# Attention over pairs of heads: values projected untransposed for two heads at once, raw weights kept where their lower parts go

## The reference

```
x = x + attn(layernorm(x), Wq, Wk, Wv, Wg, Wo)      # 8 batches, 512 tokens, 16 heads of 128
x = x + ffn(layernorm(x), ...)                      # top 128 tokens of each batch

q, k, v = h @ Wq, h @ Wk, h @ Wv ; q, k = rope(q), rope(k)      # rope: t*cos + swapped halves*sin
g_cmp, g_slc, g_swa = sigmoid(h @ Wg)                           # one gate per head and token
o_cmp = softmax over 8 block means of k, times block means of v
o_slc = softmax over the causal row, times v                    # all 8 blocks are selected
o_swa = softmax over the last 65 keys, times v
o = g_cmp*o_cmp + g_slc*o_slc + g_swa*o_swa ; return o @ Wo
```

## Time and profile before

| | us |
|---|---|
| median of 3 runs | 2504.64 |
| the profiled execution | 2504.16 |
| its span in the trace | 2502.3 |
| PE busy | 2428.0 |
| DVE busy | 1901.3 |
| POOL busy | 1584.8 |
| ACT busy | 1409.8 |

### The profile page before, as it was taken

The page is one execution under the profiler, slowest core; times in us unless marked ns, Lnnn a source line. Parts: engine busy times, 40 slices in busy tenths (PEclk is TensorE's granted clock), DMA queues, the critical chain, the costliest instruction groups (busy, mean ns, idle before and its releaser), DMA issues. The chain is left out here.

```text
span 2502.3 us, 48659 instructions
## 1 busy us (share of the span) xinstructions
PE 2428.0 (97%) x12944; PEld 2066.0 (83%) x12944; DVE 1901.3 (76%) x5863; ACT 1409.8 (56%) x3808; POOL 1584.8 (63%) x1198
## 2 busy tenths in 40 slices
PE   6999999999999999999999999999978999999998
PEld 5788888888888888888888888888867888887776
DVE  7588888888888888888888888888882777775123
ACT  7566666666666666666666666666652222213442
POOL 1777777777777777777777777777753333333442
PEclk9999999999999999999999999999989999999999
DMA  4222212121222222222222222222225333432366
GB/s 153 60 71 55 75 50 75 50 75 50 75 63 63 63 63 63 62 64 62 64 71 54 71 54 71 54 71 54 58 72 188 133 115 121 155 110 76 102 180 215
DMA packets 145681, 211.78 MB, mean 85 GB/s; under 512 B 14960, under 2 KB 56176, under 8 KB 144624
## 3 DMA queue, kind: packets, MB, share of 16 engines
q1 hardware_dynamic: 145648, 211.37, 28.9%
HBM read 93.87 MB, written 50.33 MB: 58 GB/s over the span
## 5 line engine op out<-in xcount | busy, mean ns | idle before, releaser
L526 PE MATMUL bank<-xt_hi,w_hi 128*128 (+1 forms) x1536 | 619.3, 403 | 3.0 <-PEq L170 0.8
L526 PE MATMUL bank<-xt_hi,w_lo 128*128 (+1 forms) x1536 | 600.8, 391 | 0.0
L526 PE MATMUL bank<-xt_lo,w_hi 128*128 (+1 forms) x1536 | 598.1, 389 | 0.0
L501 POOL TENSOR_TENSOR qk_lo<-s_full,qk_hi 128x512 fp32r<-128x512 f32 x256 | 330.1, 1290 | 274.9 <-ACT qk_hi L621 274.9
L489 POOL TENSOR_TENSOR cosed<-s_full,rope 128x512 f32<-128x512 f32 x256 | 330.6, 1292 | 134.0 <-ACT s_full L610 130.6
L497 POOL TENSOR_TENSOR s_full<-cosed,s_swap 128x512 f32<-128x512 f32 x256 | 333.6, 1303 | 36.7
L526 PEld LDWEIGHTS bank<-xt_hi,w_lo 128*128 128x128 f32 x1536 | 288.2, 188 | 64.1
L526 PEld LDWEIGHTS bank<-xt_hi,w_hi 128*128 128x128 f32 x1536 | 289.2, 188 | 56.6 <-DVE w_lo L138 3.5
L526 PEld LDWEIGHTS bank<-xt_lo,w_hi 128*128 128x128 f32 x1536 | 289.5, 188 | 52.7
L494 POOL TENSOR_TENSOR s_swap<-s_swap,rope 128x512 f32<-128x512 f32 x256 | 332.9, 1300 | 0.1
L626 ACT ACTIVATE pt_hi<-bank 128x384 fp32r<-128x384 f32 (+1 forms) x384 | 174.7, 529 | 260.7 <-PE bank L568 260.5
(11 more groups left out here) (166 smaller groups left out, 5416.9 us busy)
## 6 DMA issues: line engine op xcount, KB each, us to landing
s_swap<-s_full SPq DMA_DIRECT2D x512, 128.0 KB, 2.3
o_scratch<-o_sb SPq DMA_DIRECT2D x128, 256.0 KB, 2.3
o_raw<-o_scratch SPq DMA_DIRECT2D x32, 1024.0 KB, 6.3
w_raw<-in_L_ffn_W SPq DMA_DIRECT2D x64, 256.0 KB, 3.1
xin<-in_L_attn_x SPq DMA_DIRECT2D x15, 1024.0 KB, 5.5
base_scratch<-x SPq DMA_DIRECT2D x8, 1024.0 KB, 4.7
base<-base_scratch SPq DMA_DIRECT2D x32, 256.0 KB, 4.3
out<-base SPq DMA_DIRECT2D x32, 256.0 KB, 3.3
```

The lines of the kernel that those rows point to most:

```text
L501: nc.gpsimd.tensor_tensor(qk_lo[k][:], s_full[k][:], f32(qk_hi[k][:]), ALU.subtract).then_inc(lo_done[k], 1)
L526: last = nc.tensor.matmul(banks[QB[k]][:, :], w[k][:, c, :], v[:, bass.ds(b, 1), c, :], start=(n == 0), stop=(n == 3 * C - 1))
```

## The change

Units are taken in pairs of heads: pair p, then batch b, then head s of the pair, u = p*16 + b*2 + s. What is done for each is this:

- Values: in unit (b, s) the token tiles 2s and 2s+1 of the layer norm stand still and the value weights of both heads stream, 256 columns. That gives tokens by dims directly, for two tiles and two heads, in bank 7. `vt`, its copy and the four transposes are gone. `v_hi` and `v_lo` have five slots of two tiles.
- Banks: the second group of transposed probabilities goes to bank 5, not 7. TensorE waits for the evacuation of k before it and of q before the third group; the projection of values waits for the low parts of the values of the unit before.
- Rope: the cosine product is written in place, so GpSimd waits for the swapped halves first, and q is turned to its end before k. The output tile `o_sb` is now `s_swap[1]`: SyncE waits for the store before it swaps k.
- ScalarE copies the output first in its body, then empties q; the high part of q comes straight after the first row's exponentials.
- Weights: each raw tile of q and k lies where the low part goes, which is then taken in place. There are two sets (one per head of the pair), loaded once per pair in units 14 and 15; the value weights are one tile of 256 columns per chunk. VectorE splits q, GpSimd k and the values.
- Gates of all heads are stored to DRAM and loaded back 16 units at a time (`gates_dram`).
- `normalise` splits four tiles of q and k and the double tile of v on GpSimd before the attention begins, where there were three tiles.
- Loops: TensorE's loop over pairs has 16 bodies written out. The other engines have a loop over pairs with four bodies written out (`quad`), and inside it a loop of three rounds over four bodies.

```diff
+            def project_values(b, s):
+                for i in range(2):
+                    out = banks[7][:, :].rearrange("p (a i d) -> p i a d", a=2, i=2)[:, i]
+                    at = (2 * s + i) * P
+                    n = 0
+                    for c in range(C):
+                        for x, w in ((xt_hi, weights.v_hi), (xt_hi, weights.v_lo), (xt_lo, weights.v_hi)):
+                            last = nc.tensor.matmul(out, x[:, b, c, at:at + P], w[:, c, :],
+                                                    start=(n == 0), stop=(n == 3 * C - 1), skip_group_check=True)
+                            n += 1
+                last.then_inc(projected[2], 1)
...
-                    project_one(b, 2)
-                if score:
-                    pe.wait_ge(evacuated[2], u)
-                    if end:
-                        pe.wait_ge(pt_lo_done, (u - 2) * 3 + 2)
-                    for t in range(T):
-                        last = nc.tensor.transpose(banks[7][:, t * P:(t + 1) * P], vt[:, t * P:(t + 1) * P], m("ident"))
-                    last.then_inc(v_transposed, 1)
+                    pe.wait_ge(weights.v_split, p * 2 + 2)
+                    if not begun:
+                        pe.wait_ge(v_lo_done, u)
+                    project_values(b, s)
...
+            with pe.Fori(1, PAIRS) as p:
+                for k in range(4):
+                    quad(p, k)
...
 (GpSimd)
-            def turn_cos(u, k):
+            def turn(u, k):
                 pool.wait_ge(evacuated[k], u + 1)
-                nc.gpsimd.tensor_tensor(cosed[k][:], s_full[k][:], rope[:, 0, :], ALU.mult).then_inc(cos_done[k], 1)
-            def turn_sin(u, k):
                 pool.wait_ge(swapped[k], u * 32 + 32)
+                nc.gpsimd.tensor_tensor(s_full[k][:], s_full[k][:], rope[:, 0, :], ALU.mult).then_inc(cos_done[k], 1)
                 nc.gpsimd.tensor_tensor(s_swap[k][:], s_swap[k][:], rope[:, 1, :], ALU.mult).then_inc(sin_done[k], 1)
...
 (ScalarE, VectorE; GpSimd alike)
+            with act.Fori(1, PAIRS) as p:
+                quad(p - 1, 3, split=p)
+                with act.Fori(0, 3) as k:
+                    quad(p, k)
```

More of the change, by code:

```diff
@@ L56, in consts @@
     ones = np.ones((P, P))
-    misc = np.concatenate([x.reshape(P, -1) for x in (ident, causal, window, cmask, some)], 1)
+    misc = np.concatenate([x.reshape(P, -1) for x in (ident, window, cmask, some, causal)], 1)
     late = np.concatenate([before, slot, ones], 1)
@@ L63 @@
 _at = 0
-for _n, _w in (("ident", P), ("causal", P), ("window", P + WIN), ("cmask", T * NB), ("some", T)):
+for _n, _w in (("ident", P), ("window", P + WIN), ("cmask", T * NB), ("some", T)):
     MISC[_n] = (_at, _at + _w)
@@ L92, in build @@
     misc = keep("misc", [P, MISCW])
-    gates = keep("gates", [P, H * B, 3, T])
+    gates = keep("gates", [P, 2 * B, 3 * T])
     xt_at = keep.at
@@ L132, in high @@
[L132 to L138, removed]
+        self.at = r.at
+        self.hi = [[r(f"w{k}_hi{s}", [P, C, HD], F32R) for s in range(2)] for k in "qk"]
@@ L295, in _ @@
                     copy_gates(i - 1)
-            for k in range(3):
-                weights.high(act, 0, k)
+            for k, s in QK:
+                weights.high(act, 0, k, s)
+            weights.high_v(act, 0)
             place_gates(B - 2)
@@ new lines, in body, with quad, middle @@
+                if ahead is not False:
+                    weights.load_v(sp, ahead)
+            def quad(p, k, first=False, ahead=False, split=False):
+                body(p, k, 0, gate=first)
+                body(p, k, 1, ahead=ahead)
+                body(p, k, 2, split=split)
+                body(p, k, 3, split=split)
+            def middle(p):
+                with sp.Fori(1, 3) as k:
+                    quad(p, k)
+            sp.dma_start(probs[:, 0:P], misc_d[:, MISCW:MISCW + P]).then_inc(causal_loaded, 16)
@@ L501, in low @@
                 nc.gpsimd.tensor_tensor(qk_lo[k][:], s_full[k][:], f32(qk_hi[k][:]), ALU.subtract).then_inc(lo_done[k], 1)
-            def body(u, b, project, score, end, split):
-                if project:
-                    turn_cos(u, 0)
-                    turn_cos(u, 1)
-                    if split is not False:
-                        weights.low(pool, nc.gpsimd, split, 1)
-                    for part in (turn_sin, low):
-                        for k in range(2):
-                            part(u, k)
@@ L596, in body, with quad @@
                     last.then_inc(out_ready, 1)
-            def start(h):
-                head[0] = h
-            steps(pe, body, start)
+            def quad(p, k):
+                for j in range(4):
+                    body(p, k, j)
+            body(0, 0, 0, score=False, end=False)
+            body(0, 0, 1, end=False)
+            body(0, 0, 2)
+            body(0, 0, 3)
+            for k in range(1, 4):
+                quad(0, k)
+            with pe.Fori(1, PAIRS) as p:
+                for k in range(4):
+                    quad(p, k)
+            body(PAIRS, 0, 0, project=False)
+            body(PAIRS, 0, 1, project=False, score=False)
         @block.scalar
```

435 lines of the change are left out of this document (264 added, 171 removed).

## The result

The changed kernel takes 2473.14 us (median of 4 runs, 2470.11 to 2475.27). The kernel before, run beside it on the same chip, took 2504.4 (2504.12 to 2505.31). The ratio is 0.987, interval 0.9854 to 0.9885: 1.3% faster. The forecast was 2483, the range 2460 to 2510.

The account below looks back on a forecast made before the run. TensorE's instruction stream was taken as the bound, the softmax loop close behind. -27 (values) - 6 (head changes) + 4.3 (start) + 7 (jumps) = -21.7 us from 2504.16 gave 2482.5, forecast 2483, range 2460 to 2510.

Parts of the forecast that it names:

- values: TensorE's value projection: 24 matmuls of 256 columns take 2.98 us, not 3.19; -27 us over 128 units (-8 to -38).
- start of the output product: Output product's first matmul: 0.32 us might become 0.23 behind a 256-column stream; not counted, kept in the range.
- changes of head, first unit: Longer TensorE steps at 15 head changes, 10.6 us in all; with 7 pair changes instead, -6 us (0 to -10.6).
- jumps: Instruction fetch at TensorE's backward jumps over pairs: 7 jumps at 1 us each, +7 us (0 to 23).
- start: Start of the attention: barrier opens 2.7 us later and unit 0's rope chain ends later; together +4.3 us (+3 to +6).
- The second effect: The 0.09 us a unit that may go at the output product's start; widened the gain's range to -50 us.
- rival (a): More gained: all 10.6 us of long steps and 11.5 at the output product go, jumps free; 2459 us, chance 0.15.
- ScalarE's copy: ScalarE's copy of vt, 0.60 us in the softmax chain: removal gives 1.1 us room, pays only at head changes.
- Rival (c): Slower by code: VectorE's and ScalarE's inner loops fetch every four units, 22 stalls of 3.3 us; 2516 us, chance 0.13.
- Rope on GpSimd: GpSimd's new rope order ends 2.1 us before the scores need it; cost 0, but the tightest cover.
- (b): Untransposed value projection gains nothing, its 256-column matmuls lying 0.130 us apart; 2509 us, chance 0.08.
- (d): Softmax binds, so the unit stays at 13.84 us and only the start counts; 2508.5 us, chance 0.06.

Follow-up runs that it names:

- the late splits: Changed kernel with only the first head's q and k weights split on GpSimd before the barrier, the other splits in its attention program: 2468.67 us, ratio 0.9857.
- the five other runs of this start: Changed kernel, start unedited: TensorE's loop written out (2468.1 us), ScalarE's and VectorE's (2465.52), all three (2457.34), TensorE's loop turned one quad (2466.29), minimum added on VectorE (2491.75).

## Why the prediction was right in direction and ten microseconds short

By the profiled executions the change is 2473.84 - 2504.16 = -30.3 us; the forecast was -21.7. Term by term:

| term | forecast | measured |
|---|---|---|
| values | -27 | -29 (0.23 x 127) |
| start of the output product | not counted | -11.4 (0.09 x 127) |
| other hundredths in a unit | - | -2 |
| changes of head, first unit | -6 | -11 |
| jumps | +7 | +18.3 |
| start | +4.3 | +8.1 |
| behind unit 127 | 0 | -3.3 (mostly scatter) |

- **Values: right.** The distance of 0.121 us was 0.1195. The second effect, named and left out, came in full. It was an observed 0.32 against 0.23 us in the earlier trace rows, behind the same transposes whose removal was being counted, and belonged in the sum.
- **Changes of head: mis-sized.** All of the 10.6 us went, as rival (a) had it, and nothing but the jumps remains. The prediction gave two reasons, ScalarE's copy gone and fewer and thinner weight splits; which of them did it, no run separates.
- **Code: mechanism right, size wrong twice.** I counted PE's jumps alone at 1 us. They make a unit 1.46 us longer and there are six of them (the loop has seven rounds). And VectorE and ScalarE stall at their own jump over the pairs, which the sum left out altogether. Rival (c) held the price for it: a stall of 3.3 us less a room of 1.8, 1.5 us each. Found are a stall of 2.94, a room of 1.6 (0.83 us of waiting for PE and 0.76 to the scores) and 1.59 us on the path, 0.25 more than their difference. Its frequency was wrong: at the inner loops of four bodies no engine stands still, so there are six stalls and not 22. I had seen those loops and overlooked the loop around them.
- **Start: right about the barrier (73.7 said, 73.91 found), blind to what follows.** The barrier's 2.9 us and the serial rope chain's 1.4 make the 4.3. The remaining 3.8 is the lower clock. With the late splits, where it stayed at 1.00, the first mask lies 19.09 us after the first matmul (before 17.69, hence the 1.4); in the changed kernel 22.85. Ten slow matmuls behind the barrier are 10 x 0.20 = 2.0 us of it, and from the first scores to the mask it takes 3.66 us and not 2.00. By the five other runs of this start the 3.8 is at the upper end; they lie 1.6 to 3.9 us over 19.09.
- **Rope on GpSimd: right.** The low part of k ends at 1006.27, 1.8 us before the scores (2.1 said), and the weight splits fit. By the code this rests on the second set of weight tiles, which the prediction did not name: in the kernel before, without it, the same order cost 57 us.
- **ScalarE's copy: right that it pays nothing.** VectorE's wait for ScalarE fell from 1.49 to 0.74 us, not 0.6. Its wait for PE rose to 0.83, not over 1.2; the room in the softmax loop is 0.76, not 1.1. The 0.64 us from which that wait set out was read too high: one of its 98 waits is the 14.7 us of the start, and the others average 0.49. That the copy's end pays at the changes of head is not shown by itself.
- Rivals (b) and (d) fell with the distance of 0.1195 and the unit of 13.51. That the sum was only 9 us off owes something to luck, in errors of opposite sign: some 24 us more gained in the units, at the changes of head and behind unit 127, 15 us more lost at jumps and start. Of the 24, the 3.3 behind unit 127 are mostly scatter: from the last causal mask to the end it took 642.3 to 647.3 us in the kernel before and its variants, 641.5 to 644.2 in the changed kernel and its own, with next to no edit in that part.

## What to carry to other kernels

When a loop body grows so long that its instructions have to be fetched again after the jump back, count one stall for each engine that jumps back, not for the bound engine alone, and subtract only the room that the others really have. If such loops must stay, let all engines jump in the same unit, or write them out if code size allows. And when a barrier moves later, look at what the matrix engine does meanwhile: the gap can cost as much after it as in it (3.8 us and 2.9 in the run shown).

## What the runs showed of the hardware

- A stream of fp32r matmuls with a new weight tile each: 0.230 us for 512 columns, 0.1195 for 256. Halving the width costs 0.005 us a matmul. The first matmul behind a group of 128-column transposes takes 0.08 to 0.09 us more, behind a 256-column stream none.
- A jump back over a long loop, in the changed kernel: 2.9 to 3.1 us without an instruction on VectorE, 2.6 to 2.7 on ScalarE, 1.0 to 1.5 on TensorE, and in another kernel once 3.21. Jumps of several engines in one unit made that unit no longer than one of them did (14.83 to 15.19 us, against 14.97 and 15.10 on average). Straight code moved nearly as many instruction packets without these stalls.
- The granted clock in the first 30 us of the attention is not the same from run to run. After 3.40 to 3.43 us without work it fell in all six kernels with that start, and 7 to 14 matmuls came 0.43 us apart; it fell after 2.15 us in the one kernel that had that; after 0.84 us it stayed at 1.00 in all seven. After 3.07 us it stayed at 1.00 in one kernel and fell in another. The Trainium skill (TensorE: Matmul & The Clock Gate, Part 1: The HAM clock gate) calls the number of slow matmuls at the start of a kernel run-variable; the runs here agree for an idle time in its middle, and what of the 3.8 us is steady stays open.
- Two elementwise subtractions at once on VectorE and GpSimd: GpSimd's took 2.31 us, alone 1.3.
